# A four-stage transformer kernel: down projection in three bf16 parts, another order of work in the second attention

## The reference

```
q, k, v = x @ Wq.T, x @ Wk.T, x @ Wv.T          # 32 heads of 8
c = cumsum(log_sigmoid(x @ Wf.T + bf), axis=1)  # one gate a head
scores = q k / sqrt(8) + c_i - c_j, causal
o = softmax(scores) v ; y = o @ Wo.T

gate = silu((x @ w_gate) * s_gate)              # int8 weights, 256 -> 1024
up = (x @ w_up) * s_up
y = ((gate * up) @ w_down) * s_down             # int8 weights, 1024 -> 256
```

## Time and profile before

| | us |
|---|---|
| median of three runs | 1635.74 |
| the profiled execution | 1630.73 |
| its span | 1629.0 |
| TensorE busy | 1132.0 (69%) |
| VectorE busy | 1164.9 (72%) |
| ScalarE busy | 895.1 (55%) |
| GpSimd busy | 420.4 (26%) |

### The profile page before, as it was taken

One profiled execution on the slowest core, in us unless ns is written; L12 is line 12 of the kernel. 1 busy time (PEld: TensorE's weight loads), 2 busy tenths in 40 slices (PEclk: granted clock), 3 DMA queues, 4 the chain that ended last, 5 costly groups with the idle time before them and its releaser, 6 DMA issues. The chain is left out here.

```text
span 1629.0 us, 26460 instructions
## 1 busy us (share of the span) xinstructions
PE 1132.0 (69%) x7733; PEld 532.7 (33%) x7733; DVE 1164.9 (72%) x3563; ACT 895.1 (55%) x1775; POOL 420.4 (26%) x576
## 2 busy tenths in 40 slices
PE   2465555565542587878355788888888888678996
PEld 1112211221121365555234422222222222244665
DVE  4799999998967633333484688888888888476443
ACT  2688988988853233333255356666666666544121
POOL 0213122132112666666210012222222222220000
PEclk9655555555555699999768789999999999979998
DMA  1346656656534422222432511111111111120001
GB/s 58 94 100 128 137 104 124 136 109 120 111 71 136 97 67 64 66 64 67 159 118 97 173 34 50 60 54 50 54 59 52 48 59 47 55 56 1 0 14 39
DMA packets 224861, 127.66 MB, mean 78 GB/s; under 512 B 168448, under 2 KB 204416, under 8 KB 224464
## 3 DMA queue, kind: packets, MB, share of 16 engines
q1 hardware_dynamic: 204672, 100.12, 24.9%
q0 software_dynamic: 6320, 15.54, 3.0%
q10 hardware_dynamic: 13728, 10.30, 2.4%
HBM read 54.33 MB, written 37.62 MB: 56 GB/s over the span
## 5 line engine op out<-in xcount | busy, mean ns | idle before, releaser
L1793 ACT ACTIVATE qkv_made<-qkv_lower 128x1024 f32<-128x1024 f32 (+3 forms) x256 | 207.8, 867 | 111.3 <-PE qkv_lower L1617 111.2
L1958 DVE CUSTOM_DVE_ANT_0 all_y<-qkv_upper,all_mask 128x384 bf16<-128x384 f32 (+3 forms) x512 | 231.7, 485 | 35.1 <-PE qkv_upper L1581 31.2
L1581 PE MATMUL qkv_upper<-l_k,all_y 64*128 64x512 bf16 (+3 forms) x768 | 205.5, 338 | 45.1 <-DVE qkv_mx L1962 28.4
L1839 POOL TENSOR_SCALAR_AFFINE_SELECT qkv_made<-qkv_made 128x256 f32<-128x256 f32 x256 | 102.5, 406 | 436.4 <-ACT qkv_made L1793 361.8
L666 DVE CUSTOM_DVE_ANT_0 a_rows<-a_sc,all_mask 128x128 bf16<-128x128 f32 (+7 forms) x256 | 191.5, 748 | 20.9 <-PE a_sc L520 20.1
L569 ACT ACTIVATE a_rows<-a_rows 128x128 bf16<-128x128 bf16 (+7 forms) x256 | 173.2, 676 | 60.2 <-DVE a_rows L676 56.1
L1617 PE MATMUL qkv_lower<-all_y,l_k 64*128 64x384 bf16 (+3 forms) x768 | 179.3, 331 | 34.6 <-ACT qkv_made L1793 33.2
L520 PE MATMUL a_sc<-a_k,a_q 16*128 16x512 bf16 (+3 forms) x384 | 167.2, 504 | 51.7 <-DVE a_mx L666 44.7
L1962 DVE TENSOR_REDUCE qkv_mx<-qkv_upper 128x1 f32<-128x512 f32 x256 | 175.3, 685 | 10.4 <-PE qkv_upper L1581 10.2
L1636 PE MATMUL qkv_upper<-qkv_made,qkv_v_heads 128*32 128x384 f32 (+3 forms) x1920 | 179.6, 438 | 0.4
L578 ACT ACTIVATE a_unread<-a_rows 128x128 bf16<-128x128 bf16 (+7 forms) x256 | 170.6, 667 | 0.0
(11 more groups left out here) (251 smaller groups left out, 1853.9 us busy)
## 6 DMA issues: line engine op xcount, KB each, us to landing
qkv_made<-out_rows SPq DMA_DIRECT2D x16, 512.0 KB, 8.0
l_k<-k_rows SPq DMA_DIRECT2D x64, 128.0 KB
o_rows<-qkv_made SPq DMA_DIRECT2D x32, 256.0 KB, 2.0
all_y<-q_rows SPq DMA_DIRECT2D x128, 48.0 KB
a_turned_sb<-a_rows SPq DMA_TRANSPOSE x256, 2.6
a_raw<-in_gate ACTq DMA_DIRECT2D x16, 224.0 KB, 3.4
a_raw<-in_up ACTq DMA_DIRECT2D x16, 224.0 KB, 4.0
ride_wd<-in_down SPq DMA_DIRECT2D x1, 3584.0 KB, 17.4
```

Of the source, the lines that this page charges most:

```text
L1581: nc.tensor.matmul(row[:, n % SLOTS, 0:w], q_sb[of_head, u % RING, POS[qb] * P:(POS[qb] + 1) * P], k_sb[of_head, u % RING, lo:lo + w], sta ...
L1793: nc.scalar.activation(probs[:, n % GR, lo:hi], st[:, n % 2, lo:hi], ACT.Exp).then_inc(exp_done, 1)
L1958: nc.vector.tensor_tensor_reduce(out=passed[:, n % SLOTS, 0:w], in0=tile[:, 0:w], in1=mask[:, at:at + w], scale=1.0, scalar=-3e38, op0=ALU ...
```

## The change

Three parts. In the second attention the products `values(6, 7)` go from slot 11 to slot 10, and entry 3 of the rows goes ahead of `TURN`. In its opening, gates come ahead of the splits of projections 6 and 7, projections 12 to 15 go in between the first rows (with their splits on VectorE), `value(2)` and `value(3)` stand together behind the first 24 rows, and the loads of q are issued ahead of the store of c, those of k behind it. In the final stage the fused values are split into three bf16 parts and the down projection is 24 bf16 matmuls a tile instead of 8 float32 ones.

```diff
-VALUES = {1: (0,), 3: (1,), 5: (2,), 7: (3,), 9: (4, 5), 11: (6, 7)}
+VALUES = {1: (0,), 3: (1,), 5: (2,), 7: (3,), 9: (4, 5), 10: (6, 7)}
 
 
 LATER = ((12, 13), (14, 15), (16, 17), (18, 19), (20, 21), (22, 23),
-         (0, 1), (2,), (TURN, 3), (4, 5, 6), (7, 8, 9), (10, 11))
+         (0, 1), (2, 3), (TURN,), (4, 5, 6), (7, 8, 9), (10, 11))
 
...
+                sp.wait_ge(stored[j], 16 * sum(STORES[todo[i][0]] for i in range(j, half_way, pring)))
+            load_queries(0)
+            load_queries(1)
             sp.wait_ge(f_chain, 7)
             sp.dma_start(c_v[:, 0:3], cparts[:]).then_inc(c_stored, 16)
             store(half_way)
             store(half_way + 1)
-            for j in range(pring):
-                sp.wait_ge(stored[j], 16 * sum(STORES[todo[i][0]] for i in range(j, half_way, pring)))
             sp.wait_ge(c_stored, 16)
-
-            def load_unit(u):
-                load(sp, u, q_sb[:, u % RING], k_sb[:, u % RING], qk_loaded[u % RING])
-
-            load_unit(0)
+            load_keys(0)
             store(half_way + 2)
             store(half_way + 3)
-            load_unit(1)
-            for i in range(half_way + 4, len(todo)):
-                store(i)
-            for u in range(2, RING):
-                load_unit(u)
+            load_keys(1)
+            store(half_way + 4)
+            store(half_way + 5)
+            load_queries(2)
+            load_keys(2)
+            store(half_way + 6)
+            store(half_way + 7)
+            load_queries(3)
+            load_keys(3)
             for j in range(pring):
                 sp.wait_ge(stored[j], 16 * sum(STORES[todo[i][0]] for i in range(j, len(todo), pring)))
             for u in range(units):
...
-            for i in range(4, 8):
-                project(i)
+            project(4)
+            project(5)
             turn(2)
             gate(2)
+            project(6)
+            project(7)
             turn(3)
             gate(3)
-            for i in range(8, 16):
+            for i in range(8, 12):
                 project(i)
 
...
@@ -1641,15 +1652,22 @@
 
             pe.wait_ge(gates, 1)
             pe.wait_ge(xT_ready, 2 * NG)
-            for i in range(NC // 2):
-                entry(0, i)
+            for u, what in entries[:8]:
+                entry(u, what)
+            project(12)
+            project(13)
+            for u, what in entries[8:16]:
+                entry(u, what)
+            project(14)
+            project(15)
+            for u, what in entries[16:NC]:
+                entry(u, what)
             value(2)
-            for k, slot in enumerate(LATER):
-                for what in slot:
-                    entry(0 if what == TURN or what >= NC // 2 else 1, what)
-                if k == 3:
-                    value(3)
-                if TURN in slot:
+            value(3)
+            opening = [(0 if what == TURN or what >= NC // 2 else 1, what) for slot in LATER for what in slot]
+            for u, what in opening[NC // 2:]:
+                entry(u, what)
+                if what == TURN:
                     pe.wait_ge(remains, len(todo))
...
             norm_y(3)
+            copy_x(2)
             split_pair(4)
-            split_pair(6)
-            copy_x(2)
             norm_x(3)
             copy_x(3)
+            split_pair(6)
             for i in range(4):
                 gate_step(i)
...
+            maxima(16, len(entries))
+
 
 
 class Quantised:
...
@@ -2155,8 +2180,11 @@
                 if n >= 4:
                     pe.wait_ge(y_ready, n - 3)
                 for ch in range(FC):
-                    last = nc.tensor.matmul(dn[:, n % 4, 0:D], fuse[:, g % 2, ch, i * P:(i + 1) * P], wd_sb[:, ch, :],
-                                            start=(ch == 0), stop=(ch == FC - 1))
+                    if i == 0:
+                        pe.wait_ge(f_low, FC * g + ch + 1)
+                    for part in range(3):
+                        last = nc.tensor.matmul(dn[:, n % 4, 0:D], fparts[:, g % 2, part, ch, i * P:(i + 1) * P], wd_sb[:, ch, :],
+                                                start=(ch == 0 and part == 0), stop=(ch == FC - 1 and part == 2))
                 last.then_inc(dn_ready, 1)
...
+            def fuse_low(n):
+                pool.wait_ge(f_middle, n + 1)
+                nc.gpsimd.tensor_tensor(out=fparts[:, n // FC % 2, 2, n % FC, :], in0=less[:, n % 2],
+                                        in1=fparts[:, n // FC % 2, 1, n % FC, :], op=ALU.subtract).then_inc(f_low, 1)
+
             pool.wait_ge(power_set, 1)
             of_o.root(pool, 0, power)
             for g in range(1, NG):
                 of_o.root(pool, g, power)
                 of_x.root(pool, g - 1, power)
+            fuse_low(0)
             of_x.root(pool, NG - 1, power)
-            wipe(pool)
-            for g in range(NG):
-                of_y.root(pool, g, power)
+            for n in range(1, FC * NG):
+                fuse_low(n)
+                if n % FC == 0 and n // FC >= 2:
+                    of_y.root(pool, n // FC - 2, power)
+            of_y.root(pool, NG - 2, power)
+            of_y.root(pool, NG - 1, power)
 
...
+            def fuse_high(n):
+                act.wait_ge(fused, n + 1)
+                if n % FC == 0 and n // FC >= 2:
+                    act.wait_ge(dn_ready, GT * (n // FC - 1))
+                nc.scalar.copy(fparts[:, n // FC % 2, 0, n % FC, :], fuse[:, n % 2]).then_inc(f_high, 1)
+
+            def fuse_middle(n):
+                act.wait_ge(f_less, n + 1)
+                nc.scalar.copy(fparts[:, n // FC % 2, 1, n % FC, :], less[:, n % 2]).then_inc(f_middle, 1)
+
             def tanh(n):
+                if n:
+                    fuse_high(n - 1)
                 act.wait_ge(gu_ready, n + 1)
                 if n >= 2:
                     act.wait_ge(gated, n - 1)
@@ -2233,6 +2284,8 @@
                     act.wait_ge(weights.scales, 2)
                 nc.scalar.activation(th[:, n % 2, :], gu[:, n % 2, 0, :], ACT.Tanh,
                                      scale=half[:, n % FC:n % FC + 1]).then_inc(th_ready, 1)
+                if n:
+                    fuse_middle(n - 1)
...
+            def fuse_less(n):
+                dve.wait_ge(f_high, n + 1)
+                if n >= 2:
+                    dve.wait_ge(f_low, n - 1)
+                nc.vector.tensor_tensor(out=less[:, n % 2], in0=fuse[:, n % 2], in1=fparts[:, n // FC % 2, 0, n % FC, :],
+                                        op=ALU.subtract).then_inc(f_less, 1)
+
             def silu(n):
+                if n:
+                    fuse_less(n - 1)
                 dve.wait_ge(th_ready, n + 1)
                 if n >= 2:
-                    dve.wait_ge(fused, n - 1)
+                    dve.wait_ge(f_less, n - 1)
                 nc.vector.scalar_tensor_tensor(out=tmp[:, n % 2, :], in0=th[:, n % 2, :], scalar=1.0,
                                                in1=gu[:, n % 2, 0, :], op0=ALU.add, op1=ALU.mult).then_inc(gated, 1)
                 dve.wait_ge(gated, n + 1)
                 ch = n % FC
-                nc.vector.scalar_tensor_tensor(out=fuse[:, n // FC % 2, ch, :], in0=tmp[:, n % 2, :],
+                nc.vector.scalar_tensor_tensor(out=fuse[:, n % 2], in0=tmp[:, n % 2, :],
                                                scalar=both[:, ch:ch + 1], in1=gu[:, n % 2, 1, :],
                                                op0=ALU.mult, op1=ALU.mult).then_inc(fused, 1)
 
@@ -2386,6 +2450,8 @@
                     if g + 1 < NG:
                         silu(FC * (g + 1) + 2 * i)
                         silu(FC * (g + 1) + 2 * i + 1)
+                    elif i == 0:
+                        fuse_less(FC * NG - 1)
                     n = GT * g + i
                     dve.wait_ge(dn_ready, n + 1)
```

More of the change, by code:

```diff
@@ L1364, in projections, with project_and_attend @@
     return out
-def project_and_attend(nc, a, out_rows, chosen, x1, xf, spare, q_rows, k_rows, o_rows, v_units, k_sb, ident, ident_b, mask, load):
+def project_and_attend(nc, a, out_rows, chosen, x1, xf, spare, q_rows, k_rows, o_rows, v_units, k_sb, ident, ident_b, mask, load_q, load_k):
     hd = D // H1
@@ L1980, in add_max, with maxima @@
                                         in1=q_sb[:, u % RING], op=ALU.add).then_inc(row_free, 1)
-            for u, what in entries:
-                if what == TURN:
-                    add_max(u)
-                else:
-                    max_of(u, what)
-                    if what == NC - 1:
-                        parts_of_max(u)
+            def maxima(first, end):
+                for u, what in entries[first:end]:
+                    if what == TURN:
+                        add_max(u)
+                    else:
+                        max_of(u, what)
+                        if what == NC - 1:
+                            parts_of_max(u)
+            maxima(0, 8)
+            split_pair(12)
+            maxima(8, 16)
+            split_pair(14)
```

(5 more changed lines are left out.)

44 lines of the change are left out of this document (28 added, 16 removed).

## The result

Over four runs of each, the kernel before took 1638.47 us at the median and the changed one 1599.64; the ratio is 0.9764, 95% interval 0.9731 to 0.9798. The forecast against the runs shown was 1602.9. The profiled execution of the changed kernel took 1597.25, its span is 1595.4, against 1629.0. The medians differ by 38.8 us and the two spans by 33.6. The 5 us between lie in the spread of the kernel before: its profiled execution, 1630.73, is shorter than each of its four runs (1632.94 to 1641.82). What follows is read from the traces, so it places the 33.6.

What follows compares the result with a forecast made beforehand. Bound: VectorE and TensorE, neither saturated, waiting in second attention; TensorE alone in the final stage's steady part. Sum: 1630.7 − 26.1 − 6.7 + 0 = 1597.9, or 1602.9 against the runs' median; range 1589 to 1624.

Steps and rivals of the forecast that it cites:

- Values one slot earlier: Second attention: output copy and next exp start 0.89 us sooner, VectorE gains 0.85 a period, bounds 0 and 0.94.
- Turn one entry later: Second attention: add 0.55 us later, row 3's maximum ahead of it; gain 0.05 a period, bounds −0.2 and +0.6.
- Together: Second attention: values and turn orders save 0.90 us a period, 29 periods, 26.1 us; bounds −6 and +45.
- Opening: Opening of second attention: rows start 5 to 10 us earlier, same work before first add; 0, bounds −5 and +5.
- Down projection: Final stage: a tile takes 2.59 us instead of 3.45, weight loads hidden; −13.8 us for 16 tiles.
- rival D: Final stage: weight loads of the down projection do not hide, +25 us in place of −13.8, time 1641.7; chance 0.04.
- Parts of the fused values: Final stage: casts and subtractions per chunk, GpSimd's taken as 1.0 us; hidden in the steady part, paid in lead-in and last group.
- Lead-in: Start of the final stage, VectorE mostly on the chain: subtractions and casts cost +5.0 us, ends +2 and +7.
- Stall: Last group of the final stage: last subtraction queued on VectorE, then cast and GpSimd; TensorE waits, +2.1 us.
- A: Second attention: period does not fall, the two gaps are filled by each other; time 1629.0, chance 0.11.
- B: Final stage gives about 0 instead of −6.7 us, through dearer lead-in, stall, GpSimd or loads; time 1609.6, chance 0.17.
- C: Second attention slower: values(6,7) in slot 10 wait for exps or masks, rows queue behind; 1649 at 0.7 a period, chance 0.04.

Runs made afterwards that it cites:

- turn first: The changed kernel with the turn between entries 2 and 3, ahead of values(3), slots (2, TURN, 3), (4), (5, 6): 1582.19 us, ratio 0.9656.
- values alone: The kernel before with values(6,7) in slot 10 and nothing else: 1616.20 us, ratio 0.9834.
- the turn alone: The kernel before with entry 3 ahead of the turn and nothing else: 1637.82 us, ratio 0.9975.
- The two later kernels: "turn first" plus early last subtraction and seven chunks of tiles 0 and 1 ahead of the eighth, 1584.29 us; that plus value tiles among opening rows, 1581.28 us.

## Why the prediction was right

**Values one slot earlier: right, the size off by 0.11 a period.** I took 0.85 of a possible 0.94; it is 0.74. The 0.38 and 0.34 went whole, the 0.22 stayed in every kernel, even at a period of 13.43 with nothing late on ScalarE. I had put it down to the late scores because it stood behind them. TensorE's timeline of the changed kernel points at another cause, values(1), behind which the next row chunk stands; no run moved values(1), so this is argued and not shown:

```profile
1158.25 1.05 PE L1647 MATMUL qkv_upper<-qkv_made,qkv_v_heads 128*32 128x512 f32 x8
...
1159.24 0.39 PE L1592 MATMUL qkv_upper<-l_k,all_y 64*128 64x512 bf16 x1
```

That a gap comes after a stall does not make it part of it.

**Turn one entry later: right.** 0.05 forecast, 0.09 measured: the gap before the add fell to 0.62, where I had left it at 0.72. The walk (the add 0.55 later, row 3 ahead of it) describes both traces. What I did not see is what "turn first" shows: the same reasoning, carried one step on, gives 0.61. I had asked only what the change's own order wins, not what kept the transposes back: values(3).

**Together** 0.90 forecast, 0.83 measured in the steady period; 26.1 us forecast, 27.7 measured between the first and the last add. That the totals lie so near is in part luck. 29 distances at 0.83 are 24.1; one of 14.23 and the first take 0.3 back; the last is 1.3 shorter (13.48 for 14.82), where I had counted nothing; and 2.6 come from two periods of 16.20 and 16.13 of the kernel before, of which the changed one has none. I had foreseen neither of the last two.

**Opening: right at 0**, the first row chunk 12 us earlier, where I had said 5 to 10, and the first add at 936.8 in both. VectorE stands 8.77 before the row chunk that follows both value blocks, where it stood 4.93 and 2.88 behind one each.

**Down projection: right.** 2.59 forecast, 2.62 measured; −13.8 forecast, −13.3 measured. Weight loads hide, which leaves rival D out.

**Parts of the fused values: right, each a little dearer.** Lead-in +5.0 forecast, 46.2 − 41.0 = +5.2 measured; leaving the split out gives 6.0, or 5.1 counted from the reciprocal. Stall +2.1 forecast, +2.4 measured: 0.16 of it is GpSimd's subtraction, 1.16 and not 1.0. One reading under that 1.0 is wrong: the row for 4 elements in the earlier trace rows is 1.09 and not 1.01, and that instruction takes a power, so it says little of a subtraction. The stage gave 5.6, not 6.7.

**Rivals.** A fell with the period of values alone. B fell with the stage. C did not happen in slot 10; in slot 9 the kernel is slower than the changed one, but by the length of the block and not by a wait for exps. The Trainium skill's figure for an elementwise instruction of GpSimd ("GPSIMD Engine Reference", section "3.1 Elementwise — side-by-side cycle accounting"), which made 1.1 us by my estimate, was nearer than the row that I chose; the trace has 1.16.

## What to carry to other kernels

Ask of each wait on a saturated or nearly saturated engine what stood in the queue of the engine that released it: here both waits worth having, 0.74 and 0.61 us in 32 units, were a block of matmuls standing one or two places too early or too late, with all its inputs ready. Where an operand is split so that a matmul gets cheaper, price the split where no other work of the matrix engine covers it, the first and the last group, and not in the steady part. And where an instruction is appended for the last element of a pipeline, put it where its input is ready, not where the loop happens to end.

## What the runs showed of the hardware

**The clock in a steady loop.** The period of the kernel before is not always 14.87: two of its 31 distances are 16.20 and 16.13. In these TensorE's granted clock drops. The windows, columns as in the earlier trace rows, around the first:

```profile
1100.00:1110.00 10.00, 8.20 (x79) 2.89 (x78) 8.52 (x29) 6.28 (x9) 2.25 (x6) 0.93 0.11 41
1110.00:1120.00 10.00, 9.03 (x75) 2.83 (x71) 7.52 (x26) 5.99 (x9) 2.85 (x8) 0.90 0.18 53
1120.00:1130.00 10.00, 8.20 (x81) 2.56 (x78) 8.93 (x32) 6.56 (x9) 1.43 (x4) 1.00 0.17 57
```

```profile
1108.70 0.61 PE L1617 MATMUL qkv_lower<-all_y,l_k 64*128 64x512 bf16 x1 [1.06 <-ACT qkv_made L1793]
...
1124.90 0.39 PE L1617 MATMUL qkv_lower<-all_y,l_k 64*128 64x512 bf16 x1 [1.06 <-ACT qkv_made L1793]
```

The same scores of 512 columns take 0.61 at 1108.70 and 0.39 one unit later, after the same idle 1.06; the engine had worked in the same pattern for ten units. The granted clock of 0.93 and 0.90 in the two windows is a mean: full, and for part of them (0.50 from 1109 to 1112) the lower level, 1.2 GHz. It makes the unit 1.3 us longer. Such periods stand in every profile with a period of 14.87 (two to four of them) and in that of values in slot 9 (four, period 14.28), and in none of the eight with 14.78, 14.13, 14.04 or 13.43. What in the pattern decides it was not tried and stays open; the turn alone, period 14.78, has the 1.06 too and no such period.

**GpSimd and VectorE.** In the kernel with the last subtraction early, one VectorE add of two SBUF operands took 1.37 us instead of 0.42 while GpSimd subtracted, and that subtraction 1.27 instead of 1.16. The source views of the adds and of GpSimd's subtraction (shortest, median and longest, in ns), and the adds in the changed kernel:

```profile
L2404 DVE TENSOR_TENSOR all_xf<-all_xf,all_y x16: 407/420/1374, 1540.8 to 1589.5; 128x256 f32<-128x256 f32 x16
L2222 POOL TENSOR_TENSOR last_fparts<-last_less,last_fparts x32: 1148/1157/1272, 1448.5 to 1573.2; 128x512 bf16<-128x512 f32 x32
```

```profile
L2404 DVE TENSOR_TENSOR all_xf<-all_xf,all_y x16: 407/418/426, 1538.4 to 1588.5; 128x256 f32<-128x256 f32 x16
```

The two later kernels, which also have that subtraction early, show the same pair, 1.38 and 1.28; in the others no such add is longer than 0.43. VectorE's instructions with an operand in PSUM that ran beside GpSimd did not change: silu's two are at most 0.69 and 0.75 in all 32 chunks, as in the kernel before, and the second of them overlaps GpSimd's subtraction in 31. The Trainium skill ("GPSIMD Engine Reference", section "1. Specifications") says that the two share their SBUF interface and contend at VectorE instructions with two SBUF inputs; these rows agree. The slowed add ends at 1574.76, 0.28 after GpSimd's subtraction. In the changed kernel itself it costs nothing, since its own subtraction on VectorE, 0.68 to 0.69 in all 32, never meets GpSimd's.
